# One VectorE operation for the one-hots of two strips in a graph network's adjacency build

## The reference

```python
h = jnp.maximum(_layernorm(x, axis=-1), 0.0)
for l in range(5):
    agg_x = segment_sum(h[src], dst, n) + h
    agg_e = segment_sum(edge_attr @ ew.T + eb, dst, n) + eb
    h = concatenate([agg_x, agg_e], axis=1) @ w1.T + b1
    h = relu((h - mean(h, 0)) * rsqrt(var(h, 0) + 1e-5) * bn_w + bn_b) @ w2.T + b2
    if l < 4: h = relu(h)
return x + h
```

## Time and profile before

| | us |
|---|---|
| median of 3 runs | 682.5 |
| the profiled execution, whole | 680.31 |
| its span | 678.5 |
| busy: PE, PEld | 616.5, 372.9 |
| busy: DVE, ACT, POOL | 345.5, 261.6, 66.9 |
| the build, to the first layer product of line 1311 | about 256 |

### The profile page before, as it was taken

How to read it: one execution, slowest core, us unless ns; L and a number is a source line. 1 busy time by engine, 2 the same in 40 slices (tenths; PEclk the granted TensorE clock), 3 DMA queues, 4 the chain that set the end, 5 groups by cost and what they waited for, 6 DMA issues and landing times.

```text
span 678.5 us, 12888 instructions
## 1 busy us (share of the span) xinstructions
PE 616.5 (91%) x5319; PEld 372.9 (55%) x5319; DVE 345.5 (51%) x837; ACT 261.6 (39%) x569; POOL 66.9 (10%) x90
## 2 busy tenths in 40 slices
PE   4798888888999988799997999997999997999976
PEld 3676677754555544744444844446644457444456
DVE  6787999989999936530213422114321125201034
ACT  1266967754666623711113602116311127012142
POOL 5640033600110100000000000000000000000000
PEclk9787989997999998799999899998999998999999
DMA  5971000000000000010000000000100000000033
GB/s 178 326 212 8 3 28 3 5 5 4 4 2 4 5 4 3 1 31 1 1 1 1 17 17 1 1 1 1 32 1 1 1 2 1 31 1 1 1 96 95
DMA packets 13322, 19.23 MB, mean 28 GB/s; under 512 B 2263, under 2 KB 7397, under 8 KB 13251
## 3 DMA queue, kind: packets, MB, share of 16 engines
q1 hardware_dynamic: 12099, 16.00, 7.7%
q0 software_dynamic: 1152, 2.20, 1.4%
HBM read 16.26 MB, written 1.60 MB: 26 GB/s over the span
## 4 chain that ended last, share of the span: by engine, by line
PE 58%; DVE 2%; ACT 1%; issue 0%; POOLq 0%; DVEq 0%
PE bank L1281 38%; PE bank L1345 10%; PE bank L1317 8%; PE bank L1311 2%; ACT h L1398 1%; DVE bn_stats L1502 1%; DVE h L1523 0%; DVE h L1524 0%; PE bank L1328 0%; PE bank L232 0%; DVE h L1543 0%; ACT bn_small L1411 0%; DVE bn_small L1517 0%; DVE bn_small L1516 0%; DVE bn_small L1518 0%
## 5 line engine op out<-in xcount | busy, mean ns | idle before, releaser
L1281 PE MATMUL bank<-adj,h_pieces 128*128 128x504 bf16 (+1 forms) x1372 | 263.5, 351 | 0.0
L1281 PEld LDWEIGHTS bank<-adj,h_pieces 128*128 128x128 f16 x1372 | 123.0, 97 | 141.4 <-issue 10.2
L1502 DVE BATCH_NORM_STATS2 bn_stats<-bank 128x6 f32<-128x504 f32 (+1 forms) x70 | 42.8, 627 | 220.3 <-PE bank L1317 219.7
L937 ACT ACTIVATE adj<-bank 128x450 bf16<-128x450 f32 x175 | 95.8, 548 | 77.4 <-PE bank L802 66.9
L1389 ACT ACTIVATE aggT<-bank 128x504 f32<-128x504 f32 x24 | 14.2, 590 | 261.0 <-PE bank L1317 223.7
L423 DVE TENSOR_TENSOR h<-iota_lo,h 128x768 bf16<-128x768 bf16 (+1 forms) x182 | 102.1, 561 | 5.6 <-PE bank L802 5.3
L826 PE MATMUL bank<-h,adj 128*17 128x40 f32 (+11 forms) x1752 | 83.0, 206 | 15.0 <-DVE h L615 10.3
L802 PE MATMUL bank<-h 128*128 128x75 bf16 x1064 | 71.2, 204 | 16.6 <-DVE h L423 15.0
L432 PE MATMUL bank<-adj,h_pieces 128*128 128x450 bf16 x343 | 84.5, 359 | 1.6 <-issue 1.6
L802 PEld LDWEIGHTS bank<-h 128*128 128x128 bf16 x1064 | 52.7, 101 | 59.8 <-DVE h L423 43.0
L826 PEld LDWEIGHTS bank<-h,adj 128*17 128x17 f32 x1752 | 72.2, 103 | 23.1 <-DVE h L615 14.4
(11 more groups left out here) (150 smaller groups left out, 332.2 us busy)
## 6 DMA issues: line engine op xcount, KB each, us to landing
adj<-attr SPq DMA_DIRECT2D x1, 2524.5 KB
adj<-attr SPq DMA_DIRECT2D x1, 1963.5 KB
weights<-wpack SPq DMA_DIRECT2D x5, 323.0 KB
out<-h SPq DMA_DIRECT2D x6, 256.0 KB
adj<-attr SPq DMA_DIRECT2D x1, 1402.5 KB
adj<-attr SPq DMA_DIRECT2D x2, 561.0 KB
h<-mpack SPq DMA_DIRECT2D x5, 179.0 KB
adj<-order SPq DMA_DIRECT2D x2, 202.0 KB
```

The costliest lines, as they stand in the source:

```text
L937: nc.scalar.activation(out_view(u), bank_view(n % CNT_BANKS), ACT.Copy).then_inc(s_ev, 1)
L1281: last = nc.tensor.matmul(agg_ps[b][:, 0:w], hp[:, k, s, :], adj[:, k, c * LW:c * LW + w], start=(k == 0 and s == 0), stop=stop and s == p ...
L1502: V.bn_stats(stats[:, h, ds(c * 6, 6)], w1_ps[b][h][:, 0:cols]).then_inc(st_last if last and h == 1 else st_done, 1)
```

## The change

`PAIR = 2` strips share a batch. VectorE makes at every even strip the one-hots of two strips, with 1536 and 912 columns, and signals once. Each of the two buffers holds two strips; the second `lo_oh` buffer lies in the other half of `h1`. VectorE waits until the last strip of the batch two before is counted (`last_counted`). TensorE still counts strip by strip, from its part of the batch. An overflow group is a batch of its own; the strips 99 and 149 in `OV_AT` become 98 and 148, so that they are even.

To make room, the scratch of the pick moves into columns of `adj` that hold attributes of the first six row tiles (`spare`). So SyncE's loads of the ranges and GpSimd's count-up `iota_g` (now at strip 32) wait for 18 attribute steps. SyncE's two loads of the order wait for the overflow keys to be made and out, no longer for step 9. `ov_st` has one buffer, and ScalarE stages an overflow group only after the one before is added. ScalarE's `chunk_out(5)` waits for the last strip's counts, since it writes over the second `lo_oh` buffer.

```diff
-OV_AT = (56, 60, 74, 99, 124, 149, 170)
-ORDER_AFTER = 9
+PAIR = 2
+OV_AT = (56, 60, 74, 98, 124, 148, 170)
+SPARE_ROWS, LO_AT = 6, 2250
...
+def batch_at(u):
+    return u // PAIR + sum(at <= u for at in OV_AT)
+def overflow_batch(c):
+    return OV_AT[c] // PAIR + sum(at < OV_AT[c] for at in OV_AT)
+def last_counted(n):
+    for c in range(CHUNKS):
+        if overflow_batch(c) == n:
+            return overflow_at(c)
+    return max(strip_at(u) for u in range(STRIPS) if batch_at(u) == n)
...
-            lo_oh = carve(SLOTS * SG * P).rearrange("p (b x) -> p b x", b=SLOTS)
-            a_oh = carve(SLOTS * SG * AP).rearrange("p (b x) -> p b x", b=SLOTS)
+            lo_oh = [carve(PAIR * SG * P), h1[:, 1, LO_AT:LO_AT + PAIR * SG * P // 2].bitcast(BF16)]
+            a_oh = [carve(PAIR * SG * AP) for _ in range(SLOTS)]
...
                     sp.wait_ge(s_sdram, 16 * BLOCKS)
+                    sp.wait_ge(s_step, 3 * SPARE_ROWS)
...
-                    sp.wait_ge(s_step, ORDER_AFTER)
+                    sp.wait_ge(s_key, 2 * (BLOCKS + 1))
+                    sp.wait_ge(s_kout, 2 * (BLOCKS + 1))
...
                         if u == PICK_AT:
+                            pool.wait_ge(s_step, 3 * SPARE_ROWS)
+                            nc.gpsimd.iota(iota_g, [[1, CHUNK_GROUPS]], base=0, channel_multiplier=0,
+                                           allow_small_or_imprecise_dtypes=True).then_inc(s_thr, 1)
                             overflow_pairs()
...
-                            dve.wait_ge(s_cnt, n - SLOTS + 1)
-                        equal(lo_oh[:, n % SLOTS, 0:tiles * P], iota_lo, key_lo[:, g:g + tiles], P, tiles)
-                        equal(a_oh[:, n % SLOTS, 0:tiles * AP], iota_a, key_a[:, g:g + tiles], AP, tiles).then_inc(s_oh, 1)
+                            dve.wait_ge(s_cnt, last_counted(n - SLOTS) + 1)
+                        equal(lo_oh[n % SLOTS][:, 0:tiles * P], iota_lo, key_lo[:, g:g + tiles], P, tiles)
+                        equal(a_oh[n % SLOTS][:, 0:tiles * AP], iota_a, key_a[:, g:g + tiles], AP, tiles).then_inc(s_oh, 1)
...
-                        dve.wait_ge(s_kout, 2 * (block_of(u) + 1))
-                        one_hots(strip_at(u), SG * u, SG)
+                        if u % PAIR == 0:
+                            strips = min(PAIR, STRIPS - u)
+                            dve.wait_ge(s_kout, 2 * (block_of(u + strips - 1) + 1))
+                            one_hots(batch_at(u), SG * u, strips * SG)
...
-                        counts(strip_at(u), SG)
+                        counts(strip_at(u), batch_at(u), u % PAIR * SG, SG)
...
+                        if c == 5:
+                            act.wait_ge(s_cnt, strip_at(STRIPS - 1) + 1)
...
-                                if c >= 2:
-                                    act.wait_ge(s_ov, OV * (c - 1))
+                                if c >= 1:
+                                    act.wait_ge(s_ov, OV * c)
```

More of the change, by code:

```diff
@@ L288, in gin_program @@
-            dst_oh = agg0[:, tail + CW:tail + CW + DST_SLOTS * RUN * DW].rearrange("p (b x) -> p b x", b=DST_SLOTS)
-            at = tail + CW + DST_SLOTS * RUN * DW
+            sums = agg0[0:REC, 0:CW]
+            at = CW
+            dst_oh = agg0[:, at:at + DST_SLOTS * RUN * DW].rearrange("p (b x) -> p b x", b=DST_SLOTS)
+            at += DST_SLOTS * RUN * DW
             piece = agg0[0:SK, at:at + CW // 2].bitcast(BF16)
-            iota_d = agg0[:, at + CW // 2:at + CW // 2 + DW]
-            at += CW // 2 + DW
@@ L303, in gin_program @@
[L303 to L308, removed]
+            at += CW // 2
+            iota_d = agg0[:, at:at + DW]
+            assert at + DW <= 4 * CW and LO_AT >= 5 * CW
@@ L311, in gin_program, with spare @@
+            at = LO_AT + PAIR * SG * P // 2
+            ov_st = agg0[:, at:at + OV * AW // 2].bitcast(BF16)
+            assert at + OV * AW // 2 <= COLS
             words = adj_t[:, :].bitcast(I32).rearrange("p (k w) -> p k w", k=NODE_TILES)
             wordsf = adj_t[:, :].bitcast(F32).rearrange("p (k w) -> p k w", k=NODE_TILES)
+            n_ov, n_gr, o0 = OV * WIN_G, CHUNK_GROUPS, ATTR_AT // 2
+            def spare(k, a, n, view=wordsf):
+                return view[0:CHUNKS, k, o0 + a:o0 + a + n]
@@ L313, in gin_program @@
+            assert OV == 2 and 3 * n_gr <= ROW_TILES * REC and 2 * n_ov <= ROW_TILES * REC
             s0 = STAGE // 2
@@ L586, in _ @@
                         pairs(b)
-                    nc.gpsimd.iota(iota_g, [[1, CHUNK_GROUPS]], base=0, channel_multiplier=0,
-                                   allow_small_or_imprecise_dtypes=True).then_inc(s_thr, 1)
                     n = 0
@@ L793, in transposes, with counts @@
                         last.then_inc(s_tr, 1)
-                    def counts(n, tiles):
-                        pe.wait_ge(s_oh, n + 1)
+                    def counts(n, batch, first, tiles):
+                        pe.wait_ge(s_oh, batch + 1)
                         if n >= CNT_BANKS:
                             pe.wait_ge(s_ev, n - CNT_BANKS + 1)
-                        lo, a = lo_oh[:, n % SLOTS, :], a_oh[:, n % SLOTS, :]
+                        lo = lo_oh[batch % SLOTS][:, first * P:(first + tiles) * P]
+                        a = a_oh[batch % SLOTS][:, first * AP:(first + tiles) * AP]
                         for g in range(tiles):
@@ L840, in _ @@
                             if u == OV_AT[c]:
-                                counts(overflow_at(c), OV)
+                                counts(overflow_at(c), overflow_batch(c), 0, OV)
                         for b in range(1, BLOCKS):
```

22 lines of the change are left out of this document (9 added, 13 removed).

## The result

The changed kernel takes 670.18 us (median, 669.72 to 671.47), against 682.39 us (682.25 to 683.54) of the kernel before in the same comparison: ratio 0.982, 95% interval 0.9802 to 0.9839, a gain of 12.2 us. The forecast was 676.8 us with a range from 672.5. So the sign was right, the gain is twice the one worked out, and the time lies outside the range. The profiled execution took 669.72 us (span 667.9), the one of before 680.31 (678.5): 10.6 us apart. The medians are another 1.6 apart. The runs of before alone spread by 1.3 us here, and by 4 to 7 in the experiments, so nothing is read into that.

The account below looks back on a forecast made before the run. VectorE was taken to bound the build, with TensorE close behind. The terms +0.3 - 1.4 - 0.6 - 0.2 - 3.8 sum to -5.7 us, taking the median from 682.5 to 676.8; range 672.5 to 681.8 us.

Parts of the forecast that it names:

- The doubled operation: VectorE's one-hots in the build: two strips in one batch cost 1.42 us instead of 1.55, saving 0.135 us per batch.
- rival (d): One-hots in the build: the doubled operation is no cheaper than two, only costs remain, 687 us; chance 0.04.
- Rival (c): Last build stretch: longer TensorE bubbles at four overflow groups halve its clock, 690.4 us; chance 0.08.
- Strips 82 to 174: Last build stretch: TensorE's need plus overflow bubbles and GpSimd's share gives 76.1 us, gain 3.8, bounds 1.6 and 8.6.
- the overflow bubbles: Groups at strips 98, 124, 148 and 170: each costs TensorE 1.2 us, 4.8 together.
- Rival (a): Build: VectorE alone decides, so the saving counts nearly in full, 8.4 us or more, 674 us and below; chance 0.10.
- Moves costed at nothing: Moved loads, count-up and waits cost nothing; ScalarE's wait from single overflow staging is hidden, else up to 1.5 us.
- Rival (b): Build: GpSimd's additions wait twice as long beside doubled operations, so nothing is left, 681 to 682.5 us; chance 0.15.
- The start: Before strip 10: first counts come 0.65 us later, about half hidden, +0.3 us, bounds 0 and +0.65.
- Strips 68 to 82: Stretch with the order checks: 7 batches save 0.9 us, the overflow group takes most; -0.2, bounds -0.9 and +0.7.
- Strips 10 to 36: Early build: 13 batches save 1.8 us, VectorE's idle time gains nothing; -1.4 us, bounds -1.8 and 0.
- Strips 36 to 68: Mid build: sixteen batches save 2.2 us, overflow groups and TensorE's work give some back; -0.6, bounds -2.2 and +1.3.

Follow-up runs that it names:

- pair 1: Changed kernel with batches of one strip, all moves of scratch, waits and staging kept; ratio to the kernel before 0.9992 to 1.0003 in four runs.
- pairs: The changed kernel as it is, two strips per batch, against the kernel before: 670.18 us, ratio 0.982 in the first comparison.
- four single buffers: Changed kernel with four buffers of one strip instead of two of two: 688.07 us, ratio 1.0077 to the kernel before.
- the pause: Changed kernel with four one-strip buffers, VectorE also waiting after every fourth batch for its own last operation: 669.06 us, ratio 0.9939 to the kernel before.
- set B: Runs on one chip taking the changed kernel apart, with the kernel before at 672.34 us; changed kernel 663.27, with own overflow buffers 659.47.
- sets B to D: Three sets of runs, each on one chip with the kernel before, which took 672.3, 672.7 and 672.1 us there.
- set D: Runs on a fourth chip: kernel before 672.11 us, changed kernel 664.18, changed kernel with one-strip batches 672.32.
- late start: Kernel before with the low one-hot of strip 0 made twice: 679.02 us, ratio 0.9933; on another chip 673.01 us, ratio 1.0012.
- set E: Runs on a chip where the kernel before took 681.82 us; changed kernel with one-strip batches 680.89, with own overflow buffers 667.75.

## Why the prediction was right in part, and where it failed

**The doubled operation** was right to 0.01 us, and with it rival (d) falls. (The saving was rounded up: by starts it is 1.54 - 1.41 = 0.13 us a batch, 11.3 us in all.) Rival (c), slower by a clock that four bubbles spoil, falls too: the bubbles are there, one of 1.22 and three of 0.84 us, and the clock of the stretch stays at 1.00.

**Strips 82 to 174** were right, -4.0 against -3.8, and for the reasons given. The size repeats: 78.5 us in before, 78.5 in all four runs of pair 1 and 74.5 in the four profiles of pairs. Of its terms, the overflow bubbles were too dear, 3.7 us and not 4.8; the other terms must be larger by about as much, and no run parts them. Rival (a), VectorE alone, put the stretch 8.6 us lower, which is 69.9 in this cut. Three of the four bubbles taken away bring it to 71.6, so they are the larger part of what keeps it out. The measured median, 670.18 us, does lie where rival (a) put it (674 and below), but by another mechanism.

**Moves costed at nothing** were right: four times pair 1, between 0.9992 and 1.0003. ScalarE's wait for GpSimd at strip 60 never came up. It stages the second group at 126.19 after waiting for the counts, and GpSimd's additions had run from 123.04 to 124.09:

```profile
123.04 1.05 POOL L594 TENSOR_TENSOR adj<-adj,h 128x75 bf16 x2
...
126.19 0.30 ACT L960 ACTIVATE h<-bank 128x150 bf16<-128x150 f32 x1 [1.07 <-PE bank L828]
```

**Rival (b)**, GpSimd held up by VectorE, did not come here but has its mechanism, stronger than it was told. I let GpSimd wait in proportion to the length of one operation. What decides is whether VectorE ever pauses. With pairs it pauses at least at every overflow group, and the additions take 0.67 us on average (13 from 100 to 234 us), against 0.49 before. With four single buffers it doesn't pause once in the 29 us of the longest addition: 3.92 us on average, and the ratio to before is 1.0077, against 0.9939 with the pause. The two ran on different chips, and 58 us of the first one's build were at half clock, so how much of the 1.4% is GpSimd's wait itself is not told apart.

**The step that failed is the clock.** The working took the earlier trace rows's granted clocks, 0.69 at the start and 0.82 at the checks, as given, and let the clock move only in rival (c), for the worse. It moves for the better too. The measured size of what that step put at nothing: in the build of before it is halved for 30.7 us in five stretches, in that of after for 17.1 in four:

| | halved stretches in the build, us |
|---|---|
| before | 18.5-25.3, 32.1-38.9, 56.0-62.8, 86.7-90.1, 155.0-161.8 |
| after | 17.8-24.6, 55.3-58.7, 82.6-86.1, 150.9-154.3 |

13.6 us less at half clock are worth 6.8 us at most; how much of it is lost depends on whether TensorE decides there. The three parts of the sum that it spoils:

- *The start.* The step says: first counts 0.65 later, half hidden, +0.3, bounds 0 and +0.65. It left out that a stretch at clock 0.50 follows at 32 us in before and none in after. Measured -2.6. This alone is 2.9 of the 4.9 us by which the profiles differ from the forecast. The other traces of this kind of chip go with it: strip 10 is out at 41.7 to 44.6 us in the four that are at half clock for 13.7 us before it, and at 38.3 to 40.6 in the four with 6.8.
- *Strips 68 to 82.* -0.2 forecast, bounds -0.9 and +0.7; -1.2 measured. The halved stretch at the checks is 3.4 us instead of 6.8. A pair 1 run that also had only 3.4 us there (144.9 to 148.3) took 19.35 us, against 20.6 in the three with 6.8: at equal clock nearly nothing is gained, as forecast. The overflow group of strip 74 takes the saving, as the step says: with a buffer of its own for it the stretch is 17.5 us (set B).
- *Strips 10 to 36.* -1.5 for a forecast of -1.4, but partly by luck: the stretch at 56 us is 3.4 instead of 6.8. Where it is in no kernel (sets B to D) pairs win 0.4 over pair 1.

Strips 36 to 68 are at clock 1.00 in both, and the third window above, and gained 1.2 for a forecast of 0.6, within its bounds. Pairs take 49.9 there in all traces, pair 1 at undisturbed clock 50.9. Of the 2.2 us that sixteen batches save I gave too much back. The term that was wrong is the one for two overflow groups (1.0): behind the group of strip 56 TensorE waits for one-hots no longer than before, and behind that of 60 it doesn't wait in either kernel. First before, then after:

```profile
123.58 0.39 PE L802 MATMUL bank<-h 128*128 128x75 bf16 x6 [0.83 <-DVE h L423]
```

```profile
118.95 0.39 PE L828 MATMUL bank<-h 128*128 128x75 bf16 x6 [0.70 <-DVE h L443]
```

Buffers of their own for these groups gain nothing in this stretch either (50.2 us in set B). The rest, for TensorE's own work, then comes to about 1.0, where 0.6 was put.

**What remains without the start's luck.** On the chips of sets B to D no profile has a halved stretch at 30 to 40 us. Before itself was not profiled there; pair 1, which takes the same time, stands for it. Means of three profiles each:

| | to strip 10 | 10-36 | 36-68 | 68-82 | 82-174 | rest | span |
|---|---|---|---|---|---|---|---|
| pair 1 | 36.0 | 47.4 | 51.5 | 20.2 | 78.5 | 436.2 | 669.8 |
| pairs | 37.1 | 47.1 | 49.9 | 19.2 | 74.5 | 434.3 | 662.1 |
| difference | +1.1 | -0.4 | -1.6 | -1.0 | -4.0 | -1.9 | -7.7 |

In medians pairs are 9.1, 8.5 and 7.9 us below before there. The range reached down to 672.5 / 682.5 = 0.985 of before, so these three ratios (0.9866 to 0.9869) lie in it and the 0.982 of the first comparison doesn't: the miss goes with the slower start.

In the profiles the start costs something here, and more than the +0.3 forecast; with a single first batch strip 10 is out at 36.3 us, so most of that is the later first count. Two of the three pair 1 profiles have a halved stretch in strips 36 to 68 and pairs have none, so only 1.0 of the 1.6 there stands at equal clock. The -1.9 of the rest is again the clock, in work that the change doesn't touch: it is 436 us in the nine traces in which the clock is halved about 15 us behind strip 174 and again, for longer, at 32 (before and after among them), and 434 in the eleven that have one short halved stretch there. The first 50 us after strip 174, in pair 1 of set D and in pairs of set B:

```profile
233.40:283.40 50.00, 42.45 (x209) 26.91 (x209) 25.04 (x56) 22.45 (x38) 1.29 (x4) 0.90 0.01 3
```

```profile
227.10:277.10 50.00, 41.40 (x217) 26.05 (x216) 25.05 (x56) 22.33 (x39) 1.25 (x4) 0.97 0.03 8
```

**What stays open.** Why doubled batches shorten the second halved stretch on chips with the slower start, or avoid it, as pairs did in the one profile of them there is on such a chip. Depth alone doesn't do it (four single buffers had it, from 30.7 to 41.0 us, and strip 10 out at 44.0). The late start avoided it, on one chip. A plain rule "less idle before, so a better clock" fails on the rows: here are the 6.8 us ahead of the second stretch, in before and then in after. TensorE was busy for less of them in after, and only before lost its clock.

```profile
25.29:32.12 6.83, 5.37 (x110) 4.18 (x108) 3.46 (x8) 1.97 (x5) 4.74 (x5) 1.00 1.06 333
```

```profile
24.61:31.44 6.83, 5.04 (x120) 4.22 (x118) 4.71 (x10) 2.30 (x7) 2.99 (x3) 1.00 1.06 328
```

Nor is it known what sets the two kinds of chips apart. In pair 1 of set E TensorE stands still several times for reasons that the profile doesn't show, while the DMA share is full:

```profile
27.77 0.30 PE L852 MATMUL bank<-h,adj 128*17 128x24 f32 x5 [0.35 <-issue]
28.53 0.30 PE L852 MATMUL bank<-h,adj 128*17 128x28 f32 x5 [0.46 <-issue]
29.28 0.32 PE L852 MATMUL bank<-h,adj 128*17 128x4 f32 x5 [0.44 <-issue]
30.04 0.20 PE L852 MATMUL bank<-h,adj 128*17 128x40 f32 x1 [0.43 <-issue]
```

Pairs have such waits too, 3 of them with 1.8 us in all against 5 with 2.1. From 18 to 31 us all eight traces of chips with the slower start have 2 to 5 such waits of over 0.2 us, 0.8 to 2.1 us in all, and the twelve of the others none or one. That they are instructions coming late behind the attribute loads would fit, and was not tested.

## What to carry to other kernels

Read the granted clock of every stretch as a result of the kernel, not as a constant: a change that leaves TensorE's instructions as they are can give back halved stretches or bring them, on both sides of the sum, and also in stages that it doesn't touch. Put that into the range in both directions, with up to half the length of each halved stretch in the rows, and don't add what an early one gives back to the rest as if nothing followed: here later stretches took much of it. When a ring of buffers is coarsened, look at the small group that takes one of its buffers: here a buffer of its own for it was worth another 3.8 us over the changed kernel (set B). Test the depth of the ring apart from the length of the operations. And before making VectorE's stream gapless, look who on GpSimd needs its gaps.

## What the runs showed of the hardware

- A GpSimd addition of about 0.4 us took 29.12 us beside a VectorE that ran its two-input one-hots back to back, and ended when VectorE stopped. With one wait of VectorE for itself in every fourth batch the mean of these additions was 0.58 us instead of 3.92 (on another chip).
- The cost of such an operation on VectorE is a straight line up to 1536 columns: 0.86 us between starts, with 0.53 ns a column and 0.06 us fixed taken from shorter ones.
- One program took 682 us on two chips and 672 on three (one set of runs on each), and a change worth 0.7% on one of the first kind (0.9933) was worth nothing on one of the second (1.0012). A gain of this size must be compared on one chip, and better on two.
- With instructions unchanged, the work behind strip 174 took 436 us where TensorE's clock was halved for 10.2 us in its first 50 us, and 434 where it was for 3.4.
